# Two key tiles a run in the last attention layer, with a ring of three weight slots and the residual kept in device memory

## The reference, cut to what matters

```
x = L0(x)   # two small attentions with 32 latent channels
x = L1(x)   # attention with 32 query/key channels, residual
x = L2(x)   # group norm, one head of 256 channels, projection, residual
x = L3(x)   # group norm, 8 heads of 32 channels, projection,
            # layer norm over channels, residual
```

```
h      = group_norm(x, 32 groups)
q,k,v  = h @ wq.T + bq, h @ wk.T + bk, h @ wv.T + bv      # 8 heads of 32
probs  = softmax(q k^T / sqrt(sqrt(32)))                  # 1024 x 1024 per head
out    = layer_norm(concat(probs v) @ wo.T + bo) + x      # x: the residual
```

## Time and profile before

| | |
|---|---|
| median of 3 runs | 2777.87 us (2777.54 to 2778.6) |
| profiled execution | 2775.3 us, of it 2773.5 us span |
| granted TensorE clock, mean | 0.941 of full speed |
| PE busy | 2573.6 us, 93% |
| DVE busy | 1887.9 us, 68% |
| ACT busy | 1286.2 us, 46% |
| POOL busy | 590.9 us, 21% |
| DMA | 72.15 MB, mean 26 GB/s |

### The profile page before, as it was taken

How to read it: one execution, slowest core, us unless ns; L and a number is a source line. 1 busy time by engine, 2 the same in 40 slices (tenths; PEclk the granted TensorE clock), 3 DMA queues, 4 the chain that set the end, 5 groups by cost and what they waited for, 6 DMA issues and landing times.

```text
span 2773.5 us, 26540 instructions
## 1 busy us (share of the span) xinstructions
PE 2573.6 (93%) x9892; PEld 1411.0 (51%) x9892; DVE 1887.9 (68%) x1925; ACT 1286.2 (46%) x2209; POOL 590.9 (21%) x322
## 2 busy tenths in 40 slices
PE   7989988999999999999999999999999999888887
PEld 4456654464645556364554646445563545543332
DVE  4544228686578866787586875777667875778885
ACT  3353222646345552645426463455626454144555
POOL 0082130050100401031010501104020320124473
PEclk8999997989999999999999899999999999989898
DMA  2000001010202002020200102020020201122200
GB/s 89 1 1 1 1 7 39 20 27 1 76 1 46 1 31 46 1 46 1 59 18 6 41 1 76 1 46 1 12 65 1 46 1 31 31 46 46 46 1 31
DMA packets 29297, 72.15 MB, mean 26 GB/s; under 512 B 10224, under 2 KB 10416, under 8 KB 28912
## 3 DMA queue, kind: packets, MB, share of 16 engines
q1 hardware_dynamic: 29168, 70.45, 10.2%
HBM read 11.40 MB, written 8.39 MB: 7 GB/s over the span
## 4 chain that ended last, share of the span: by engine, by line
PE 73%; DVE 17%; ACT 5%; issue 3%; POOL 1%; DMA 0%; DVEq 0%; SPq 0%; ACTq 0%; POOLq 0%
PE ps L633 11%; PE ps L666 10%; PE ps L652 9%; PE ps L784 8%; PE ps L954 7%; PE ps L875 6%; PE ps L641 6%; PE ps L788 4%; DVE ba_nmx L1335 3%; PE ps L722 2%; PE ps L861 2%; DVE fa_nmx L1335 2%; DVE accb L1503 2%; DVE bb_nmx L1335 1%; DVE tmp L1384 1%
## 5 line engine op out<-in xcount | busy, mean ns | idle before, releaser
L1188 ACT ACTIVATE prb<-ps 128x512 f32<-128x512 f32 x896 | 490.1, 602 | 316.0 <-PE ps L666 285.6
L1335 DVE TENSOR_REDUCE ba_nmx<-ps 128x1 f32<-128x1024 f32 x448 | 531.1, 1219 | 115.5 <-PE ps L652 113.7
L1503 DVE TENSOR_TENSOR accb<-accb,prb 128x1024 f32<-128x1024 f32 x312 | 392.9, 1288 | 107.1 <-ACT prb L1188 105.9
L666 PE MATMUL ps<-qs,ks 97*128 97x512 f32 x896 | 357.8, 474 | 30.9 <-DMA qs<-ba_nmx_r 16.0
L652 PE MATMUL ps<-ks,qs 96*128 96x512 f32 x896 | 335.0, 475 | 16.2 <-DVE ba_nmx L1335 14.9
L1049 ACT ACTIVATE pr<-ps 128x512 f32<-128x512 f32 x336 | 197.2, 601 | 315.9 <-PE ps L875 236.7
L555 POOL TENSOR_TENSOR q2k<-pr,q2k 128x512 fp32r<-128x512 f32 x112 | 143.7, 1299 | 812.4 <-ACT q2k L1086 812.4
L666 PEld LDWEIGHTS ps<-qs,ks 97*128 97x128 f32 x896 | 160.2, 197 | 277.8 <-ACT prb L1188 167.9
L954 PE MATMUL ps<-prb,vb 128*32 128x512 f32 x1792 | 251.1, 634 | 2.5 <-ACT prb L1188 2.5
L652 PEld LDWEIGHTS ps<-ks,qs 96*128 96x128 f32 x896 | 177.6, 208 | 122.8 <-DVE ba_nmx L1335 51.5
L545 POOL TENSOR_TENSOR acc<-pr 128x1024 f32<-128x1024 f32 x28 | 67.2, 2398 | 747.0 <-ACT pr L1049 626.6
(11 more groups left out here) (320 smaller groups left out, 3564.3 us busy)
## 6 DMA issues: line engine op xcount, KB each, us to landing
qs<-part SPq DMA_DIRECT2D x168, 128.0 KB, 2.5
ks<-part SPq DMA_DIRECT2D x168, 128.0 KB, 2.5
xm<-in_x SPq DMA_DIRECT2D x8, 1024.0 KB, 5.7
out<-prb SPq DMA_DIRECT2D x28, 256.0 KB, 2.2
q2k<-part SPq DMA_DIRECT2D x48, 128.0 KB, 2.4
w<-in_weights SPq DMA_DIRECT2D x1, 2592.0 KB, 8.7
out<-pr SPq DMA_DIRECT2D x4, 256.0 KB, 2.0
qs<-ba_nmx_r SPq DMA_DIRECT2D x56, 4.0 KB, 1.8
```

The lines of the kernel that those rows point to most:

```text
L666: return pe.matmul(o.ps[:, bank, :], keys[0:ROW + 1, tile(jt)], queries[0:ROW + 1, cols(ic)], start=True, stop=True)
L1188: act.activation(weights3(o, s, g), o.ps[:, turn3[score_use(s, g) % 3], :], ACT.Exp)\
L1335: dve.tensor_reduce(o.nmx[:, head, it:it + 1], o.ps[:, bank:bank + 2, :], AX.XY, ALU.max, negate=True).then_inc(o.max_sb[n].sem, 1)
L1503: dve.tensor_tensor(o.sums[pair], o.pairs[(s - 1) % 2][pair] if j == 1 else o.sums[pair], o.pairs[s % 2][pair], ALU.add).then_inc(done.sem, 1)
```

## The change

Layer 3 weighs two key tiles in one run of eight matmuls instead of one tile in four; the weights have three slots instead of two; room for the third slot comes from `xm`, which has two buffers instead of three. As the third slot of `prb` also takes in the residual at the end, the image after layer 2 is written to device memory (`kept`) when its back begins, its buffer gets the next image but one as soon as the group norm has read it, and the residual is read back from `kept` when the second last run is weighed. All `ORDER` tables are new. The diff below goes through tables and tiles, then SP, PE, ACT and DVE. (Lines are those of before unless said otherwise; in the new file L954 is L974, L666 is L687, L652 is L673, L633 is L654, L788 is L809.)

```diff
+RUN = 2
+RING = 3
 ORDER = {
     ("fronts", "PE"): (
-        2, 3, 4, 1, 5, 1, 1, 1, 2, 2, 4, 1, 1, 1, 1, 1, 5, 1, 2, 1, 2, 1, 2, 2, 1, 2, 1, 1, 1, 1, 1, 2, 1, 3,
+        2, 3, 3, 1, 5, 1, 1, 1, 1, 1, 2, 1, 2, 1, 2, 1, 3, 1, 2, 1, 6, 2, 1, 1, 2, 3, 1, 1, 2, 1, 1, 1, 1, 1,
...
-        xm = [sb(f"xm{n}", [P, CH, T]) for n in range(3)]
+        xm = [sb(f"xm{n}", [P, CH, T]) for n in range(2)]
+        kept = nc.dram_tensor("kept", (B, C, T), F32, kind="Internal").ap().rearrange("b (h p) t -> b p h t", p=P)
-        prb = sb("prb", [P, 2, QUAD, IW])
+        prb = sb("prb", [P, RING, QUAD, IW])
...
-            back_lane("bb", [B - 1], 0, h[:], q2k2[:, 0:QUAD, :], q2k2[:, QUAD:, :], tokens(xm[B % 3]),
-                      [[pr[:, 0:2, :], pr[:, 2:4, :]], [acc[:], tmp[:]]],
+            back_lane("bb", [B - 1], 0, h[:], q2k2[:, 0:QUAD, :], q2k2[:, QUAD:, :], tokens(xm[B % 2]),
+                      [[pr[:, 0:2, :], pr[:, 2:4, :]], [acc[:], tmp[:]],
+                       [xm[(B - 1) % 2][:, ch, :].rearrange("p (i n) -> p i n", i=IC) for ch in range(CH)]],
...
+        def residual(o, ch):
+            return o.pairs[2][ch]
...
                 def back(b):
+                    sp.wait_ge(front_of(b).res[2].sem, front_of(b).res[2].at(b, 4))
+                    sp.dma_start(kept[b], xm[b % 2][:]).then_inc(o.kept.sem, 16)
+                    yield
+                    if b + 2 < B:
+                        sp.wait_ge(o.gn[3]["h"].sem, o.gn[3]["h"].at(b, CH))
+                        sp.wait_ge(o.kept.sem, o.kept.at(b, 16))
+                        sp.dma_start(xm[b % 2][:], x_v[b + 2]).then_inc(x_loaded[b % 2].sem, 16)
+                    yield
...
+                    sp.wait_ge(o.kept.sem, o.kept.at(b, 16))
+                    sp.wait_ge(o.weighed[3].sem, o.weighed[3].at(b, CH * STEPS3 // RUN - 1))
+                    for pair in range(2):
+                        sp.wait_ge(o.summed3[pair].sem, o.summed3[pair].at(b, (NT - 1) * IC * CH - 2))
+                    for ch in range(CH):
+                        sp.dma_start(residual(o, ch), kept[b, :, ch, :].rearrange("p (i n) -> p i n", i=IC)).then_inc(o.again.sem, 16)
+                    yield
                     for ic in range(IC):
-                        if ic and b + 3 < B:
-                            sp.wait_ge(o.l3_g.sem, o.l3_g.at(b, 4))
-                            sp.dma_start(xm[b % 3][:], x_v[b + 3]).then_inc(x_loaded[b % 3].sem, 16)
...
-                        def weigh(s):
-                            ic, jt = divmod(s, NT)
-                            n = STEPS3 * u + s
-                            pe.wait_ge(o.exped[3].sem, o.exped[3].at(b, QUAD * (n + 1)))
-                            if jt == 0 and n:
+                        def weigh(first):
+                            n = STEPS3 * u + first
+                            pe.wait_ge(o.exped[3].sem, o.exped[3].at(b, QUAD * (n + RUN)))
+                            if first % NT == 0 and n:
                                 pe.wait_ge(o.taken[3].sem, o.taken[3].at(b, n // NT))
-                            for g in range(QUAD):
+                            for s in range(first, first + RUN):
+                                jt = s % NT
+                                for g in range(QUAD):
...
                         for s in range(STEPS3):
                             yield from scores(s, 0)
-                            if s:
-                                weigh(s - 1)
+                            if s and s % RUN == 0:
+                                weigh(s - RUN)
                                 yield
                             yield from scores(s, 1)
...
-                            if n >= 2 and g == 2 * pair:
-                                act.wait_ge(o.weighed[3].sem, o.weighed[3].at(b, n - 1))
-                                chunk, j = divmod(n - 2, NT)
+                            if n >= RING and g == 2 * pair:
+                                act.wait_ge(o.weighed[3].sem, o.weighed[3].at(b, (n - RING) // RUN + 1))
+                                chunk, j = divmod(n - RING, NT)
...
                     yield from both_rounds(maxima, middle, steps)
+                    dve.wait_ge(o.again.sem, o.again.at(b, 16 * CH))
...
-                                                     scalar=vcol("ln_w", ch), in1=xm[b % 3][:, ch, cols(ic)],
+                                                     scalar=vcol("ln_w", ch), in1=residual(o, ch)[:, ic, :],
```

More of the change, by code:

```diff
@@ L360, in back_lane @@
                 alone(kind, IC * CH) for kind in ("total", "logged", "inverse", "taken", "normed"))
-            o.ones = alone("ones", 16)[3]
             o.stacked = [alone(f"stacked{g}", 16 * 6 * CH)[3] for g in range(QUAD)]
-            o.l3_proj, o.l3_y, o.l3_sq, o.l3_n, o.l3_g, o.l3_out = (
-                alone(f"l3_{kind}", 4)[3] for kind in ("proj", "y", "sq", "n", "g", "out"))
+            o.stacked[0].before = 16
+            o.l3_proj, o.l3_sq, o.l3_n, o.l3_g, o.l3_out = (
+                alone(f"l3_{kind}", 4)[3] for kind in ("proj", "sq", "n", "g", "out"))
             o.l3_var = alone("l3_var", IC)[3]
@@ L368, in back_lane @@
             o.stored = alone("stored", 16 * 4)[3]
+            o.kept, o.again = alone("kept", 16)[3], alone("again", 16 * CH)[3]
             group_norm_of(o, in_turn, 3)
@@ L379, in attention_layers @@
         setup_products = signal("setup_products")
-        x_loaded = [Signal(semaphore(f"x_loaded{n}"), list(range(n, B, 3)), 16) for n in range(3)]
+        x_loaded = [Signal(semaphore(f"x_loaded{n}"), list(range(n, B, 2)), 16) for n in range(2)]
         fronts = (
@@ L469, in _ @@
             sp.dma_start(cst[:], constants).then_inc(loaded.sem, 16)
-            for b in range(3):
+            for b in range(2):
                 sp.dma_start(xm[b][:], x_v[b]).then_inc(x_loaded[b].sem, 16)
@@ L585, in back @@
                                 pool.wait_ge(done.sem, done.at(b, (NT - 1) * n + j - 1))
-                            pool.tensor_tensor(o.sums[1], o.pairs[(s - 1) % 2][1] if j == 1 else o.sums[1],
-                                               o.pairs[s % 2][1], ALU.add).then_inc(done.sem, 1)
+                            pool.tensor_tensor(o.sums[1], o.pairs[(s - 1) % RING][1] if j == 1 else o.sums[1],
+                                               o.pairs[s % RING][1], ALU.add).then_inc(done.sem, 1)
                             yield
@@ L818, in layer1 @@
                     pe.wait_ge(o.l0_res.sem, o.l0_res.at(b, 4))
-                    yield from queries_and_keys01(b, 1, xm[b % 3])
+                    yield from queries_and_keys01(b, 1, xm[b % 2])
                     for half in range(2):
@@ L978, in steps @@
                                 yield
-                        weigh(STEPS3 - 1)
+                        weigh(STEPS3 - RUN)
                         yield
@@ L1151, in front @@
                     yield from chunks(b, 1)
-                    yield from group_norm(b, 2, xm[b % 3], o.h, 0)
+                    yield from group_norm(b, 2, xm[b % 2], o.h, 0)
                     for which, bias, dst in ((0, "bq2", o.qh2), (1, "bk2", o.kh2)):
@@ L1165, in back @@
                 def back(b):
-                    yield from group_norm(b, 3, xm[b % 3], o.hb, 0)
+                    yield from group_norm(b, 3, xm[b % 2], o.hb, 0)
                     def queries_and_keys(blk):
@@ L1201, in back @@
                     if b == B - 1:
-                        act.wait_ge(backs[0].l3_g.sem, backs[0].l3_g.at(B - 3, 4))
+                        act.wait_ge(backs[0].gn[3]["h"].sem, backs[0].gn[3]["h"].at(B - 2, CH))
+                        act.wait_ge(backs[0].kept.sem, backs[0].kept.at(B - 2, 16))
                     take_values(b, 3, 0, o.vb, 0)
@@ L1387, in chunks @@
                             dve.wait_ge(o.normed[n].sem, o.normed[n].at(b, CH * ic + ch + 1))
-                            dve.scalar_tensor_tensor(out=xm[b % 3][:, ch, cols(ic)], in0=o.tmp[:, ch, :], scalar=vcol(bias, ch),
-                                                     in1=xm[b % 3][:, ch, cols(ic)], op0=ALU.add, op1=ALU.add)\
+                            dve.scalar_tensor_tensor(out=xm[b % 2][:, ch, cols(ic)], in0=o.tmp[:, ch, :], scalar=vcol(bias, ch),
+                                                     in1=xm[b % 2][:, ch, cols(ic)], op0=ALU.add, op1=ALU.add)\
                                 .then_inc(o.res[n].sem, 1)
@@ L1502, in add_weights @@
                                 dve.wait_ge(done.sem, done.at(b, (NT - 1) * n + j - 1))
-                            dve.tensor_tensor(o.sums[pair], o.pairs[(s - 1) % 2][pair] if j == 1 else o.sums[pair],
-                                              o.pairs[s % 2][pair], ALU.add).then_inc(done.sem, 1)
+                            now = STEPS3 * u + s
+                            dve.tensor_tensor(o.sums[pair], o.pairs[(now - 1) % RING][pair] if j == 1 else o.sums[pair],
```

(4 more changed lines are left out.)

71 lines of the change are left out of this document (34 added, 37 removed), and 49 rows, old and new, of the table ORDER.

## The result

The changed kernel takes 2715.2 us (median of four runs, 2712.4 to 2716.8) where the kernel before, beside it, takes 2777.7; the ratio is 0.9775, 95% interval 0.9758 to 0.9792. One execution of a kernel shown further down (twelve idle matmuls) took 4406.8 us at a granted clock of 0.74 and is left out of its time.

What follows compares the result with a forecast made beforehand. PE was taken to bound the six "both" parts, PE and DVE alternating in the last; -27.9 - 4.7 + 8.8 - 7.4 = -31.2 on the profiled 2775.3 gives 2744.1, as a median 2747 us, range 2730 to 2771.

Steps and rivals of the forecast that it cites:

- (a): Six "both" parts: half the visits to 32-column work, 15 fewer per part at 0.31 us each, saves 27.9 us.
- (c): New order, second round: PE's 2.68 us wait for `shift_in` grows by 1.46 us per round, costing 8.8 us.
- (d): New order, group norm: PE's 1.24 us wait for `hb` goes, saving 7.4 us over six.
- (b): "Backs", the last stage: visits to 32-column work fall from 68 to 38; half of 9.3 us taken, 4.7 saved.
- (e): Exponentials' waits for runs in "both": counted as nothing, bound 84 us; third slot can only help in "backs", not counted.
- (f): DMAs: the image's extra store and loads stay hidden, counted as nothing; 34 us if the stacks did not hide them.
- More than forecast: Rival, 2727 us, chance 0.09: "backs" gives 9.3, the `shift_in` wait does not grow, slow stretches shorten.
- The order gives the time back: Rival, 2764 us, chance 0.19: PE's work shrinks but waits grow, with PE at lower clock behind them.
- nothing to be told: Rival, 2778 us, chance 0.06: the back lane's own chain, not PE's work, sets each part.
- slower: Rival, 2861 us, chance 0.06: a run of eight does not stream (0.04), or DMAs delay the stacks (0.02).

Runs made afterwards that it cites:

- old_order_2_slots: Kernel after with single weighs, two-slot wait and the order tables of before; image buffers, store, loads and SP's table stay new: 2775.8 us, 0.9992 of before.

## Why the prediction was right in sign and half the size

By stages, the six "both" parts gained 45.6 us where 26.5 were forecast, the last stage 18.3 where 4.7 were, and the fronts lost 5.4, for which there was no term.

**What bounds it: right.** PE did set the parts, and less work for PE shortened them. A run streams, 1.85 us where the bound was 2.2. The Trainium skill, "TensorE: Matmul & The Clock Gate", Part 3, The mechanism, has the rule that weight loads overlap running matmuls only where the row group differs, and beside it names a second way for a load to go ahead, into a background weight buffer. By the rule alone a run would have taken 2.9, an estimate of the prediction; this trace does not agree, now for one lane and one bank too, and which other way the loads take no run here shows. One reading was off: the rest of PE's idle time was not all "in pieces below half a microsecond", as single waits reached 0.7 us (L788), and 6.2 us of it were the exponentials above.

**(a), the step that failed.** "A visit saved is worth 0.12 + 0.19 = 0.31 us", times fifteen, times six: this took a visit to have a price that does not depend on the list it stands in. As a price of PE's work it was nearly right in the new list: at the full clock, an estimate that counts a stretch at half the clock as half lost, weighs and scores of an equal part fall from 83.5 to 79.3 us, 4.2 where 4.65 were forecast, 0.28 a visit. In the old list the same visits save 1.8 us, 0.12 each. But what a part gains or loses is settled elsewhere: the same runs cost 88 us in the old order and save 71 in the new one. Means of the five equal parts, three slots unless said otherwise (PE's waits over 0.15 us; what PE loses to the lower clock while it works; the rest, its work at the full clock):

| us | length | waits | lost to the clock | work |
|---|---|---|---|---|
| before (two slots) | 324.9 | 12.7 | 10.6 | 301.6 |
| old order, single | 324.3 | 11.8 | 11.5 | 301.0 |
| old order, runs | 338.0 | 20.3 | 19.2 | 298.5 |
| new order, single | 329.0 | 14.7 | 14.9 | 299.4 |
| after | 318.3 | 11.4 | 11.7 | 295.2 |

Runs save PE's work in both orders (2.5 and 4.2 us); in the old one waits and the clock behind them take 16.2 back, in the new one they give 6.5 more. That was priced in two waits only, (c) and (d). So of the 6.6 us that an equal part gained, 4.2 are visits, 0.3 those two waits, and 2.1 were in no term.

**(b) and (e), the last stage: mis-sized in kind.** "I take half, 4.7 us" for the visits, and the third slot "can only help in 'backs'; not counted". The stage gained 18.3: the visits 2.5, the third slot 8.4, the new tables 7.5. The sign was there to be read in the last stage of before. PE waited 18.4 us there for exponentials (13.5 ahead of scores, 4.9 ahead of weighs; the 16.3 of the expectations are the longest rows alone), and ACT's exponentials in turn 25.1 us for a slot to be summed (22.7) or weighed (2.4); the longest rows of both:

```profile
PE ps L666 <- ACT acc L1188: 4.5, 1, 4.5
PE ps L666 <- ACT pr L1188: 4.4, 6, 2.5
PE ps L666 <- ACT prb L1188: 3.5, 7, 1.2
PE ps L954 <- ACT prb L1188: 2.5, 2, 2.2
...
  POOL w L586: 7.0, 5
  DVE w L1503: 6.0, 5
```

With the third slot alone (old order, single weighs) the 25.1 are 2.8 and the 18.4 are 8.0; in after 5.0 and 2.1. I had named the slot and left its wait unpriced. The 8.4 us are not simply these waits: other waits of PE grew in their place, and less time was lost to the lower clock; how the two divide it stays open. In "both" the zero of (e) held, but only because of the third slot: with two, the exponentials of the kernel with runs hold PE up by 45.1 us in the five equal parts, which are 128 us longer,

```profile
PE ps L688 <- ACT prb L1212: 45.1, 77, 2.0
```

and the kernel takes 195 us more.

**(c) and (d): nearly right.** The wait of the second round was to grow from 2.68 to 4.1 us; it is 2.73 + 0.97 = 3.7, as two waits. The wait for `hb` is gone. **(f): right**, at nothing, by old_order_2_slots; the load had 4.8 us to spare where 3 were reckoned.

**The first "both" part** was forecast like the others and gained 12.5 us. By the same three steps: third slot 1.9, new order -4.1, runs 14.7; its clock rose from 0.89 to 0.91, and by the same estimate 6.5 us less are lost to it and PE's work is 7.3 us less, while the waits grew by 1.3. Why the clock rose there stays open.

**The rivals.** "More than forecast" was the right side, at 2727 still 12 us short, and for other reasons: its shorter slow stretches did not come (the clock of the equal parts is 0.95 to 0.97, before 0.96 to 0.97), its 9.3 us for the last stage came twice over. "The order gives the time back" is true of the new order without runs, 22.7 us lost with three slots, and "nothing to be told" and "slower" are what runs do without the new order; I weighed these as single outcomes, not as what each part does without the others.

What stays open: how the 2.1 us without a term come about. At the full clock PE's projections (L654) fell by 1.3 us in an equal part and its maxima (L673) by 1.0 with no change in their work, and each by 0.8 already with the new tables and single weighs, so a part of it comes with the tables; waits other than the two fell by 1.0, and 1.1 more is lost to the clock. No run takes these apart.

## What to carry to other kernels

When a change comes with a new order, don't price its edits on the old one and add: with the edit alone, the order alone and both, the sign can differ each time, and three cheap runs tell. Before taking work off the bounding engine, look what waits that work covers in the other lanes, and where the trace shows a slow stretch behind such a wait, price the wait with it and not by its length. And don't leave a buffer slot at nothing where waits end on it: here 25.1 us of waits for a slot stood ahead of exponentials in the last stage, and the third slot gave that stage 8.4.

## What the runs showed of the hardware

- A gap of PE of 1.35 us was followed by 8.2 us at a granted clock of 0.58, one of 0.29 us by none; filled with idle matmuls, the same place ran at 1.00. The Trainium skill, "TensorE: Matmul & The Clock Gate", "Why this matters for your kernels", says that idle gaps between bursts of matmuls put the clock back; the trace agrees, though this gap is shorter than those that the page warns of.
- The length of a gap alone does not tell. The 1.24 us for `hb` in before were followed by 8.2 us at 1.00, and 0.85 us in the old order with runs (L784, 1210.8) by 8 us at 0.57; why, no run here shows:

```profile
1041.84:1050.00 8.16, 8.16 (x22) 4.20 (x23) 2.52 (x4) 3.18 (x5) 0.00 (x0) 1.00 0.00 0
...
1210.85:1218.85 8.00, 8.00 (x24) 2.26 (x24) 4.68 (x5) 0.68 (x2) 0.00 (x0) 0.57 0.00 0
```

- An idle f32 matmul of 320 columns takes 0.55 us (twelve 6.6 us, in 24 records), one of 256 columns about 0.5 (three in 1.5 us).
- A load of 1 MB took 5.7 us and takes 4.8 in after; the store of the same size 4.2.
